# Graph layer on one core: one product for the vector part of z of two tiles, in front of both messages

## The chip, the cores and the metric

The kernel runs on one core of a Trainium2 chip. Its time is the device time of one execution in microseconds (us). "TensorE" is PE in the rows (its weight loads are PEld), "VectorE" is DVE, "ScalarE" is ACT, "GpSimd" is POOL; SP issues transfers. All data are 32-bit floats.

## The reference

One layer of a graph network over 50,000 nodes of 160 features (64 scalars and 32 vectors of 3) and 50,000 edges, sorted by their destination, then a residual and a layer norm:

```python
h = silu(edge_scalars @ (Wfc1 / sqrt(FC_IN)));  w = h @ (Wfc2 / sqrt(FC_H))   # w0..w3 per edge
e0 = f0[edge_src];  e1 = f1[edge_src]           # node features through Wl1_0, Wl1_1
mid0 = w0 * e0 * sh0
mid1 = w3 * einsum('eum,em->eu', e1, sh1) / sqrt(3.0)
mid2 = w1[:, :, None] * e0[:, :, None] * sh1[:, None, :]
mid3 = w2[:, :, None] * e1 * sh0[:, :, None]
# means over the edges of each destination, n0..n3
alpha = scal @ Wa * a * inv96
out_s = scal @ Wl2_s * a * inv96
out_v = einsum('num,uv->nvm', vec, Wl2_v) * a[..., None] * inv96
x = layernorm(x + sc + alpha * concat(out_s, out_v))
```

The kernel applies the last matrices per edge, ahead of the means. The message of an edge has 161 numbers: its share of alpha, 64 scalars and 96 numbers of the vectors. The vectors' share with sh1 is one row of 32 numbers times the three components of sh1: that is the vector part of z.

## The kernel before, in words

The first stage makes the messages. A tile is 128 edges, one on each partition; two tiles (t = 0, 1) are a pair (k), two pairs are a quad (q), 98 quads in all. Step d of the stage works on several quads at once, each engine in its own fixed order, with semaphores between the engines:

- GpSimd gathers the node rows of quad d, four indirect transfers (L587), each pair's behind the transposes of the quad four steps back that read the same slot of `gat`.
- TensorE: `first_layer(d)` (L670), `turn(d, 0)` (transposes, L676 and L678), `combine(d-3, 0)`, `turn(d, 1)`, `combine(d-3, 1)`, then `weigh(d-1)`. `combine` makes y of a pair, for each tile a product at L733 and one at L736, tile 0 first. `weigh` makes e (L696, L702) and w (L715).
- ScalarE: for each pair `take_turned(d, k)` (h_sb at L830, t_sb at L832) and `take_second(d-3, k)`, which copies 65 numbers of y of each tile to z (L840), one copy for each tile. At the end it copies e to e_sb (L855).
- VectorE: `multiply(d-2, 0)` (mid = w times e_sb, L977), `label(d-3)` (L985), `finish(d-3, 0)`, `multiply(d-2, 1)`, `finish(d-3, 1)`, `prepare(d+2)` (L952, L961, L967), and in some steps one small operation that prepares the second stage (`between`).
- SP stores the messages of each quad to DRAM.

`finish(q, k)` makes the messages of a pair. For each tile it waits for ScalarE's copy, writes the other 96 numbers of z (L995) and adds z to y times sh0 (L1001), which is the message. `y` of pair 0 lies in PSUM banks 2 and 3, which are also those of e, so `weigh` has these waits in front of L696:

```python
pe.wait_ge(t_out, 2 * q + 2)
for t in range(2):
    if q >= 2:
        pe.wait_ge(msg_ready[t], 2 * (q - 2) + 1)
    if q >= 1:
        pe.wait_ge(e_out[t], q)
```

`y` of pair 1 has banks of its own. z has one slot for each of the four tiles of a quad, `msg` two halves of a quad each.

The second stage takes the nodes in 98 groups of 512. For each it loads the windows of messages from DRAM, sums them by destination with one-hot matrices (L795), and adds the node's own product, the residual and the norm. Its first loads are issued by SP during the first stage, the others as the groups advance.

Of the kernel before, what the change touches and what calls it, by code (L numbers as in the profile page):

```python
# [22 lines left out]
P = 128  # L23
F32 = mybir.dt.float32
I32 = mybir.dt.int32
ALU = mybir.AluOpType
# [3 lines left out]
MUL0, MUL1 = 64, 32  # L30
# [65 lines left out]
def gnn_kernel(nc, turned, spread, x_g, src_t, dst_t, dst_rows, sh_t, ea_t, weights, out):  # L96
# [22 lines left out]
    with ExitStack() as ctx:  # L119
        def sb(name, shape, dt=F32):  # L120
            return ctx.enter_context(nc.sbuf_tensor(name, shape, dt))

        def sem(name):
            return ctx.enter_context(nc.semaphore(name))
# [54 lines left out]
        sha = sb("sha", [P, SHA_RING, QUAD, 4])  # L179
# [5 lines left out]
        z = sb("z", [P, 2, 2, 1 + D])  # L185
# [106 lines left out]
        mid_ready = [sem(f"mid_ready{t}") for t in range(2)]  # L292
        y_ready = [sem(f"y_ready{t}") for t in range(2)]
        zc_ready = [sem(f"zc_ready{t}") for t in range(2)]
        zb_ready = [sem(f"zb_ready{t}") for t in range(2)]
        label_ready = sem("label_ready")
        msg_ready = [sem(f"msg_ready{t}") for t in range(2)]
        messages_out = [sem(f"messages_out{h}") for h in range(2)]
# [634 lines left out]
        def _(dve):  # L933
# [54 lines left out]
            def finish(q, k):  # L988
                p, ring, y = 2 * q + k, q % SHA_RING, y_ps[k]
                for t in range(2):  # L990
                    n = 2 * k + t
                    dve.wait_ge(zc_ready[t], p + 1)
                    if p >= 2:
                        dve.wait_ge(msg_ready[t], p - 1)
                    nc.vector.tensor_tensor(  # L995
                        z[:, k, t, 1 + MUL0:].rearrange("p (m v) -> p m v", m=3),
                        y[:, t, 0:MUL1].unsqueeze(1).broadcast_to([P, 3, MUL1]),
                        sha[:, ring, n, 1:4].unsqueeze(2).broadcast_to([P, 3, MUL1]),
                        ALU.mult).then_inc(zb_ready[t], 1)
                    dve.wait_ge(zb_ready[t], p + 1)  # L1000
                    nc.vector.scalar_tensor_tensor(  # L1001
                        out=msg[:, q % 2 * QUAD + n, 0:1 + D], in0=y[:, t, Y_A:Y_C],
                        scalar=sha[:, ring, n, 0:1], in1=z[:, k, t, :],
                        op0=ALU.mult, op1=ALU.add).then_inc(msg_ready[t], 1)

            def step(d):
                if alive(d, 2):
                    multiply(d - 2, 0)
                if alive(d, 3):
                    label(d - 3)  # L1010
                    finish(d - 3, 0)
                if alive(d, 2):
                    multiply(d - 2, 1)
                if alive(d, 3):
                    finish(d - 3, 1)
                if alive(d, -AHEAD):
                    prepare(d + AHEAD)
# [459 lines left out]
```

## Time and the profile before

| | us |
|---|---|
| median of 3 runs (lowest, highest) | 932.42 (932.19, 933.69) |
| the profiled execution | 932.28 |
| its span in the trace | 930.5 |

The profiled execution is one run of the program; all rows are of it. Times in rows are counted from the start of its span. The first stage fills about 550 us of it, the second the rest. In a timeline each row is a start, a duration, the engine, the line and the operation; in brackets stands how long the engine was idle before it and what ended that.

### The profile page before, as it was taken

How to read it: one execution, taken by the hardware profiler on the slowest of the kernel's cores; microseconds unless marked ns; L12 is line 12 of the kernel's file. 1: busy time of each engine (PE TensorE's matmuls, PEld its weight loads, DVE VectorE, ACT ScalarE, POOL GpSimd, SP SyncE). 2: the span in 40 equal slices, each digit the busy share in tenths (PEclk: the TensorE clock that was granted, in tenths of full speed). 3: DMA queues.
4: the chain of work that ended last, by engine and by line, in shares of the span. 5: the costliest groups of instructions: out<-in, count | busy, mean ns of one | idle time of the engine just before them, and what ended most of it. 6: DMA issues, size and time to landing. Idle time of an engine off the chain costs nothing.

```text
span 930.5 us, 27956 instructions
## 1 busy us (share of the span) xinstructions
PE 880.9 (95%) x8336; PEld 758.5 (82%) x8336; DVE 812.1 (87%) x2797; ACT 632.5 (68%) x1961; POOL 714.5 (77%) x804
## 2 busy tenths in 40 slices
PE   3899999999999999999999889999999999999995
PEld 2778887888877878888888779989999898899994
DVE  3789999999988999999999978888888888888887
ACT  1555555555654555565565547888988888988887
POOL 6777777777777776777777318989998888989894
PEclk9999999999999999999999999999999999999998
DMA  6465554455565555456544227999999999999993
GB/s 181 118 178 159 163 143 127 133 140 131 140 133 133 168 156 150 132 160 181 153 131 133 86 84 231 305 305 302 303 302 301 300 304 295 300 306 308 304 298 136
DMA packets 87522, 186.47 MB, mean 200 GB/s; under 512 B 17647, under 2 KB 48139, under 8 KB 87372
## 3 DMA queue, kind: packets, MB, share of 16 engines
q1 hardware_dynamic: 48411, 87.72, 29.1%
q10 hardware_dynamic: 20016, 61.15, 19.7%
q0 software_dynamic: 18944, 35.81, 17.8%
q8 instruction: 69, 1.13, 0.5%
q14 instruction: 82, 0.66, 0.2%
HBM read 119.66 MB, written 64.95 MB: 198 GB/s over the span
## 4 chain that ended last, share of the span: by engine, by line
PE 46%; POOL 22%; issue 17%; DVE 11%; DMA 3%; ACT 1%; POOLq 0%; DVEq 0%; ACTq 0%
PE ps L795 7%; POOL res L640 7%; PE ps L736 7%; POOL gat L587 6%; PE ps L715 5%; POOL xa L628 5%; PE ps L733 4%; PE ps L805 4%; PE ps L696 4%; PE ps L702 4%; DVE mid L977 3%; PE ps L678 3%; POOL xa L624 3%; DVE z L995 2%; DMA gat<-spread,srcs 2%
## 5 line engine op out<-in xcount | busy, mean ns | idle before, releaser
L587 POOL DMA_INDIRECT gat<-turned,srcs x196 | 190.8, 973 | 66.6 <-issue 61.8
L587 POOL DMA_INDIRECT gat<-spread,srcs x196 | 188.7, 963 | 61.8 <-issue 60.0
L855 ACT ACTIVATE e_sb<-ps 128x512 f32<-128x512 f32 x196 | 106.4, 595 | 123.1 <-PE ps L702 122.0
L795 PE MATMUL ps<-win,hot 60*128 60x162 f32 x2352 | 189.1, 306 | 0.7 <-DVE hot L1318 0.7
L736 PE MATMUL ps<-wy,mid 128*128 128x161 f32 x784 | 182.3, 314 | 0.0
L795 PEld LDWEIGHTS ps<-win,hot 60*128 60x128 f32 x2352 | 164.9, 186 | 17.1 <-issue 16.5
L1001 DVE SCALAR_TENSOR_TENSOR msg<-ps,sha,z 128x161 f32<-128x161 f32 x392 | 151.0, 385 | 14.0
L640 POOL TENSOR_TENSOR res<-agg,pre 128x640 f32<-128x640 f32 x98 | 152.2, 1553 | 9.9 <-ACT agg L900 9.9
L733 PE MATMUL ps<-wy,mid 128*128 128x97 f32 x784 | 141.6, 262 | 0.2 <-DVE mid L977 0.2
L977 DVE TENSOR_TENSOR mid<-ps,e_sb 128x512 f32<-128x512 f32 x196 | 133.2, 680 | 2.2 <-PE ps L715 2.2
L878 ACT ACTIVATE fin<-res,shift,rstd 128x160 f32<-128x160 f32 x292 | 132.2, 539 | 1.3 <-DVE shift L1267 1.3
L900 ACT ACTIVATE agg<-ps,coef 128x160 f32<-128x160 f32 x392 | 122.8, 409 | 6.3 <-DVE coef L1358 6.2
L733 PEld LDWEIGHTS ps<-wy,mid 128*128 128x128 f32 x784 | 123.5, 191 | 1.3 <-issue 0.7
L840 ACT ACTIVATE z<-ps 128x65 f32<-128x65 f32 x392 | 89.7, 229 | 46.0 <-PE ps L736 45.5
L736 PEld LDWEIGHTS ps<-wy,mid 128*128 128x128 f32 x784 | 119.2, 192 | 0.0
L805 PE MATMUL ps<-wy,xt 128*128 128x128 f32 x784 | 113.5, 288 | 0.4 <-DVE pre L1345 0.4
L805 PEld LDWEIGHTS ps<-wy,xt 128*128 128x128 f32 x784 | 94.9, 191 | 17.7 <-issue 17.5
L995 DVE TENSOR_TENSOR z<-ps,sha 128x96 f32<-128x96 f32 x392 | 97.9, 250 | 9.1 <-ACT z L840 2.5
L830 ACT ACTIVATE h_sb<-ps 128x128 f32<-128x128 f32 x196 | 54.4, 278 | 74.3 <-PE ps L678 64.7
L715 PE MATMUL ps<-h_sb,wt 64*128 64x256 f32 x784 | 102.0, 379 | 1.4 <-DVE mid L977 1.4
L628 POOL TENSOR_TENSOR xa<-xin 128x512 f32<-128x512 f32 x98 | 102.8, 1048 | 0.0
L832 ACT ACTIVATE t_sb<-ps 128x384 f32<-128x384 f32 x196 | 95.0, 485 | 0.0
(104 smaller groups left out, 1543.2 us busy)
## 6 DMA issues: line engine op xcount, KB each, us to landing
win<-rows SPq DMA_DIRECT2D x392, 114.6 KB
rows<-msg SPq DMA_DIRECT2D x98, 326.0 KB
out<-fin ACTq DMA_DIRECT2D x47, 640.0 KB, 5.4
xin<-x_g ACTq DMA_DIRECT2D x92, 322.0 KB, 4.4
gat<-turned,srcs POOLq DMA_INDIRECT x196
gat<-spread,srcs POOLq DMA_INDIRECT x196
eas<-ea_t SPq DMA_DIRECT2D x7, 384.0 KB, 4.8
xin<-x_g SPq DMA_DIRECT2D x6, 322.0 KB, 4.2
```

The source lines that it names most:

```text
L587: pool.indirect_dma_start(out=gat[:, slot, first:first + of.shape[1]], out_offset=None, in_=of, in_offset=bass.IndirectOffsetOnAxis(ap=src ...
L628: nc.gpsimd.tensor_tensor(xa[:, b0, 0:GROUP, :], xin[:, n, :, 1:1 + P], xin[:, n, :, 0:1].broadcast_to([P, GROUP, P]), ALU.mult).then_inc( ...
L640: nc.gpsimd.tensor_tensor(res[:, slot], agg[:, b3], pre[:, b3], ALU.add).then_inc(res_ready, 1)
L715: last = nc.tensor.matmul(w_ps[:, t, 2 * c * P:2 * (c + 1) * P], wt[half, w:w + P], h_sb[half, b].rearrange("p k e -> p (k e)"), start=Tru ...
L733: nc.tensor.matmul(y[:, t, 0:W_Y1 - W_YA], mid[:, q % 2, t, 0, k, :], wy[:, 0:W_Y1 - W_YA], start=True, stop=True)
L736: nc.tensor.matmul(y[:, t, W_Y1 - W_YA:YW], mid[:, q % 2, t, 1, k, :], wy[:, of:of + VEC + 1 + MUL0], start=True, stop=True).then_inc(y_re ...
L795: last = nc.tensor.matmul(agg_ps[b1][:, 2 * h + k, 0:SW], hot[side(h), b1, k, c, :], win[side(h), (b - 1) % RING, k, c, 0:SW], start=c == ...
L805: nc.tensor.matmul(sca_ps[:, k, :], xt[:, b1, k, :], wy[:, W_SA - W_YA:W_SB - W_YA], start=True, stop=True)
L878: last = nc.scalar.activation(fin[:, past, k, :], res[:, past, k, :], ACT.Identity, bias=shift[:, past, k:k + 1], scale=rstd[:, past, k:k ...
L900: last = nc.scalar.activation(agg[:, b0, k, :], agg_ps[b0][:, k, 1:1 + D], ACT.Copy, scale=coef[:, b0, k:k + 1])
L977: nc.vector.tensor_tensor(mid[:, q % 2, t].rearrange("p c k e -> p (c k e)"), w_ps[:, t], e_sb[:, t], ALU.mult).then_inc(mid_ready[t], 1)
L1001: nc.vector.scalar_tensor_tensor(out=msg[:, q % 2 * QUAD + n, 0:1 + D], in0=y[:, t, Y_A:Y_C], scalar=sha[:, ring, n, 0:1], in1=z[:, k, t, ...
```

## The change

The two products that write the vector part of z, one for each tile, become one product over both tiles of a pair. It stands behind the waits for both of ScalarE's copies and in front of both messages. The semaphore that told of each product, one for each tile, becomes one for both.

```diff
-        zb_ready = [sem(f"zb_ready{t}") for t in range(2)]
+        zb_ready = sem("zb_ready")
...
                 for t in range(2):
-                    n = 2 * k + t
                     dve.wait_ge(zc_ready[t], p + 1)
                     if p >= 2:
                         dve.wait_ge(msg_ready[t], p - 1)
-                    nc.vector.tensor_tensor(
-                        z[:, k, t, 1 + MUL0:].rearrange("p (m v) -> p m v", m=3),
-                        y[:, t, 0:MUL1].unsqueeze(1).broadcast_to([P, 3, MUL1]),
-                        sha[:, ring, n, 1:4].unsqueeze(2).broadcast_to([P, 3, MUL1]),
-                        ALU.mult).then_inc(zb_ready[t], 1)
-                    dve.wait_ge(zb_ready[t], p + 1)
+                nc.vector.tensor_tensor(
+                    z[:, k, :, 1 + MUL0:].rearrange("p t (m v) -> p t m v", m=3),
+                    y[:, :, 0:MUL1].unsqueeze(2).broadcast_to([P, 2, 3, MUL1]),
+                    sha[:, ring, 2 * k:2 * k + 2, 1:4].unsqueeze(3).broadcast_to([P, 2, 3, MUL1]),
+                    ALU.mult).then_inc(zb_ready, 1)
+                for t in range(2):
+                    n = 2 * k + t
+                    dve.wait_ge(zb_ready, p + 1)
                     nc.vector.scalar_tensor_tensor(
                         out=msg[:, q % 2 * QUAD + n, 0:1 + D], in0=y[:, t, Y_A:Y_C],
```

## Rows read from the trace of the kernel before

**Rows 1.** The page, part 1: busy time, share of the span and instructions.

```profile
PE 880.9 (95%) x8336; PEld 758.5 (82%) x8336; DVE 812.1 (87%) x2797; ACT 632.5 (68%) x1961; POOL 714.5 (77%) x804
```

**Rows 2.** The table by stretches: PE, PEld, DVE, ACT, POOL, clock, DMA share, GB/s.

```profile
300.00:400.00 100.00, 97.39 (x870) 81.29 (x868) 93.23 (x273) 58.38 (x190) 72.71 (x76) 1.00 0.54 152
```

**Rows 3.** The waits of the first stage: us in total, times, longest.

```profile
PEld ps L696 <- ACT t_sb L832: 29.3, 90, 0.7
DVE sha L952 <- DMA gat<-spread,srcs: 21.2, 9, 11.6
PE ps L696 <- DVE msg L1001: 12.8, 25, 2.2
```

**Rows 4.** The timeline of VectorE in an ordinary step, label to mid.

```profile
301.70 0.17 DVE L985 COPY msg<-dsts 128x4 f32<-128x4 f32 x1
302.01 0.26 DVE L995 TENSOR_TENSOR z<-ps,sha 128x96 f32<-128x96 f32 x1
302.31 0.39 DVE L1001 SCALAR_TENSOR_TENSOR msg<-ps,sha,z 128x161 f32<-128x161 f32 x1
302.61 0.25 DVE L995 TENSOR_TENSOR z<-ps,sha 128x96 f32<-128x96 f32 x1
302.89 0.38 DVE L1001 SCALAR_TENSOR_TENSOR msg<-ps,sha,z 128x161 f32<-128x161 f32 x1
303.19 0.68 DVE L977 TENSOR_TENSOR mid<-ps,e_sb 128x512 f32<-128x512 f32 x1
```

**Rows 5.** The timeline of TensorE in the same step, and the next L696.

```profile
301.69 0.47 PE L736 MATMUL ps<-wy,mid 128*128 128x161 f32 x2
302.00 0.27 PE L676 MATMUL ps<-ident,gat 128*128 128x128 f32 x1
...
303.02 0.47 PE L736 MATMUL ps<-wy,mid 128*128 128x161 f32 x2
303.53 0.66 PE L696 MATMUL ps<-t_sb,wt 64*64 64x256 f32 x8
...
308.75 0.66 PE L696 MATMUL ps<-t_sb,wt 64*64 64x256 f32 x8
```

**Rows 6.** The timeline of ScalarE: copies of pair 0, last copy of pair 1.

```profile
301.75 0.23 ACT L840 ACTIVATE z<-ps 128x65 f32<-128x65 f32 x1
302.20 0.23 ACT L840 ACTIVATE z<-ps 128x65 f32<-128x65 f32 x1 [0.22 <-PE ps L736]
...
308.74 0.23 ACT L840 ACTIVATE z<-ps 128x65 f32<-128x65 f32 x1 [0.22 <-PE ps L736]
```

**Rows 7.** The timeline of VectorE in a longer step.

```profile
328.52 0.15 DVE L985 COPY msg<-dsts 128x4 f32<-128x4 f32 x1
328.59 0.24 DVE L995 TENSOR_TENSOR z<-ps,sha 128x96 f32<-128x96 f32 x1
...
329.45 0.38 DVE L1001 SCALAR_TENSOR_TENSOR msg<-ps,sha,z 128x161 f32<-128x161 f32 x1
```

**Rows 8.** The timeline of TensorE, the L696 of that step.

```profile
330.09 0.66 PE L696 MATMUL ps<-t_sb,wt 64*64 64x256 f32 x8 [0.27 <-DVE msg L1001]
```

**Rows 9.** The timeline of ScalarE, the last t_sb ahead of it.

```profile
329.03 0.48 ACT L832 ACTIVATE t_sb<-ps 128x384 f32<-128x384 f32 x1
```

**Rows 10.** The timeline of GpSimd: the gather behind the longer gap, and another.

```profile
301.98 0.94 POOL L587 DMA_INDIRECT gat<-turned,srcs  x1 [0.52 <-issue]
303.23 0.95 POOL L587 DMA_INDIRECT gat<-spread,srcs  x1 [0.30 <-issue]
```

**Rows 11.** The timeline of TensorE: first regular and last L696, 95 steps apart.

```profile
33.80 0.66 PE L696 MATMUL ps<-t_sb,wt 64*64 64x256 f32 x8 [1.13 <-DVE msg L1001]
...
542.04 0.66 PE L696 MATMUL ps<-t_sb,wt 64*64 64x256 f32 x8 [0.32 <-DVE msg L1001]
```

**Rows 12.** Groups by line and shape, 200 to 300 us: busy us, mean ns.

```profile
L961 DVE TENSOR_TENSOR qprod<-gat,sha 128x384 f32<-128x384 f32 x18 | 10.0, 558 | 2.2 <-DVE sha L952 0.5
```

**Rows 13.** The table by stretches, behind a gather that landed late.

```profile
281.00:286.00 5.00, 4.94 (x33) 4.00 (x34) 3.50 (x10) 1.72 (x4) 3.48 (x4) 0.66 0.54 141
```

## The prediction

> **What bounds the kernel now.** I read the page first. TensorE is busy for 95% of the span, VectorE for 87%, GpSimd for 77% [rows 1], which names no bound: the kernel has two stages with different limits. The table by stretches shows that the change lies wholly in the first, where in 300 to 400 us TensorE is busy 97.4, VectorE 93.2 and GpSimd 72.7 of 100 us, with the clock granted in full [rows 2]. Three nearly full engines need the question which wait ends last, so I went to the waits. In the first stage almost all of TensorE's waits stand before one line, L696, the start of the second-layer products `weigh` [rows 3]: its weight load waits 90 times, 29.3 us in all, put down to ScalarE's `t_sb`; its matmul waits 25 times, 12.8 us, for VectorE's `msg`.
>
> Which of the two is it? The timelines settle that. In an ordinary step the second message of `finish(q, 0)` starts at 302.89 and takes 0.38, so it ends at 303.27 [rows 4]; L696 starts at 303.53 [rows 5], 0.26 later. In a longer step the message ends at 329.45 + 0.38 = 329.83 [rows 7] and L696 starts at 330.09 [rows 8], again 0.26 later, while `t_sb` had ended at 329.03 + 0.48 = 329.51 [rows 9], 0.58 before. The distance to the message is constant, so L696 always waits for the message, also where the profile names `t_sb`: `e` shares its PSUM banks with `y` of pair 0, and `weigh` waits until both messages of pair 0 have read it.
>
> Now the loop that sets a step. TensorE needs 0.31 from the start of a pair of L736 to its next instruction (301.69 to 302.00), and the last pair in front of L696 starts at 303.02 [rows 5], so L696 could begin at 303.33; TensorE stands idle for 0.20. VectorE waits as well: the label copy starts at 301.70 and z of tile 0 only at 302.01, 0.31 later, just behind ScalarE's copy that ends at 301.75 + 0.23 = 301.98 [rows 4, 6]. In the longer step, where VectorE has other work in front, the same two are 0.07 apart (328.52 to 328.59) [rows 7]. So VectorE waits 0.24 of every ordinary step for ScalarE, ScalarE waits for TensorE's combine, and TensorE waits 0.20 for VectorE's messages. No engine is the bound; a loop through three of them is, and it is 308.75 - 303.53 = 5.22 us long [rows 5]. VectorE's own work is 5.22 - 0.24 = 4.98 a step, TensorE's 5.22 - 0.20 = 5.02. GpSimd's four gathers stand 1.25 apart and one of them has 0.52 before it instead of 0.30, so it needs 5.22 - 0.22 = 5.00 [rows 10].
>
> Between the first regular L696 at 33.80 and the last at 542.04 [rows 11] there are 95 steps. Counted there: 62 of about 5.22 (the loop), one of 4.66 at the end, 20 between 5.25 and 5.46 with a mean of 5.39 and 7 up to 5.62 with a mean of 5.54 (steps where VectorE prepares the second stage), and 5 longer ones, mostly behind gathers that landed late.
>
> **The change part by part.** Every pair of tiles now has two z products of 96 numbers, each directly in front of its message. They become one product of 192, with both messages behind it.
>
> VectorE's occupancy. Now z, msg, z, msg start at 302.01, 302.31, 302.61, 302.89 and the next operation at 303.19: 1.18 for a pair [rows 4]. The trace has no z of 192. Below it lies z of 96 with 0.25 to 0.26 [rows 4]; above it twice that, 0.50, since one operation shouldn't cost more than the two it replaces; between them the product of 384 numbers with a broadcast factor and the same kind of four-dimensional pattern takes 558 ns [rows 12]. From 250 to 558 ns for 288 more numbers is 1.07 ns each, so 96 more give 0.25 + 0.10 = 0.35. I take 0.35: one operation and its rows on both sides agree with one slope. The first message starts about 0.04 after z has ended (302.01 + 0.26 to 302.31 [rows 4]), the second, which has nothing to wait for, 0.30 after the first, as the z behind a message does now (302.31 to 302.61), and the next operation 0.30 later again: 0.39 + 0.30 + 0.30 = 0.99 in place of 1.18. That is 0.19 less for a pair, 0.38 for a step, and VectorE's own time falls from 4.98 to 4.60. If the second message were held until the first has ended it would start 0.385 behind it, not 0.30; no row shows a message directly behind a message, so this stays as an upper bound of 0.09 a step.
>
> The Trainium skill speaks for this bound: VectorE: DVE Perf Modes, "The DRAIN you can't avoid", has the next operation wait until the pipeline is empty, and only excepts operations that are not held. The rows have the next operation start before the last one's end (302.31 + 0.39 = 302.70 against 302.61 [rows 4]), so I go by the rows; by the rule without its exception the sum would be 95 times 0.09, some 8 us, higher.
>
> The wait that it adds. The product now needs the copies of both tiles. ScalarE's copy of tile 0 ends at 301.98, that of tile 1 starts at 302.20, after 0.22 of waiting for TensorE's combine of tile 1, and ends at 302.20 + 0.23 = 302.43 [rows 5, 6]. VectorE is through with the label at about 301.77, so the start of z moves from 302.01 to 302.46. What is queued behind it on VectorE is both messages of pair 0, then `mid` and pair 1; for the messages TensorE waits at L696. From the end of the copy of tile 1 to L696 it is now 303.53 - 302.43 = 1.10. After: 0.03 to the start of z, 0.35 of z, 0.04, 0.30 between the messages, 0.38 of the second, 0.26 to L696, 1.36 in all. The loop closes through this copy, because the copy follows TensorE's combine (L736 of tile 1 at 301.69 [rows 5]), which follows the last L696 in TensorE's own order with no wait between. So the loop becomes 5.22 + 0.26 = 5.48.
>
> Pair 1 costs nothing. Its second copy is ready 308.74 + 0.23 - 303.53 = 5.44 after the L696 of the step before [rows 5, 6], its z can only start about 5.74 after it, behind the later `mid`; the 0.19 saved there vanishes in VectorE's wait for pair 0, which grows to some 0.9. `mid` itself starts 0.26 later against ScalarE and TensorE of the same step, and its readers are a step away. GpSimd follows TensorE's transposes and gets 0.48 of slack instead of 0.22, SP's stores get more time. The one z semaphore instead of two adds no wait: both messages wait for the same product.
>
> The sum: 62 steps x 0.26 = 16.1. In 20 steps 5.48 - 5.39 = 0.09 each, 1.8: there VectorE's extra work now hides in its own longer wait (4.60 plus at most 0.6 of extra stays below 5.48). In 7 steps 5.48 - 5.54, -0.4. In the five long ones a gather has up to half a us more lead, so I take -1, with ends of 0 and -3. The last quads, where the loop is open, +0.3. Together +16.8 us. The second stage starts when the messages are done and its queue of loads is released by the same step counters, so it moves as a whole. Against the profiled execution of 932.28 us (span 930.5), which stands 0.14 below the median of 932.42, that is 949.1; forecast 949 us.
>
> **Rivals.** (a) Forecast: the loop grows by what the second copy costs less what the fused product saves, 949 us, between 940 (z of 0.25) and 957 (second message held). Chance 0.80.
>
> (b) Faster: VectorE's occupancy is what sets the step, and 0.38 of it goes. Then the step falls until TensorE's 5.02 ends it: -0.20 x 95 = -19, 913 us. For it: VectorE is busy 93%, and the longer steps are its own. Against it: the 0.24 before z in every ordinary step. It decides if the second copy is ready before VectorE arrives, which needs it 0.66 earlier than the rows have it. Chance 0.07. This is where a rule of the Trainium skill stands, VectorE: DVE Perf Modes, "Rules for kernel authors": with chained operations it is their number that is to be kept small, not the semaphores; this kernel would lose 196 of them. The trace doesn't contradict it for VectorE's time, only that this time sets the step.
>
> (c) No change: the copies close up. The balance is zero when the start of z moves by no more than the 0.19 that the fusion saves for pair 0; the rows have it move by 0.45. TensorE's two combines would have to stand closer than 0.5, and nothing in the change does that. 932 us, chance 0.04.
>
> (d) Worse: the held second message together with a z of 0.50, +0.24 more a step, or a lower TensorE clock from its longer idle of 0.46 a step. Behind the longest idle before L696, 2.2 us [rows 3], the mean granted clock of 281 to 286 us was 0.66 of 2.4 GHz [rows 13], between its two levels: those 5 us do the work of 3.3, so each such fall would cost 1.7 us, and ten of them 17. But the 90 idle times of 0.7 at most left the clock full where I looked [rows 2, 3]. 960 to 975 us, chance 0.09.
>
> **The numbers.** A change of less than 0.2% can't be told from none here. Slower holds (a) and (d), 0.89; faster 0.07; same 0.04. The range of 80% lies within the slower cases: 939 from z at 0.25 (10 us less) and 958 from the held message, which leaves out (b), (c), most of (d).
>
> **What would show it.** Steps of 5.48 between starts of L696 where they were 5.22, and the 5.4 ones gone; z of 128x192, some 350 ns, starting 0.03 behind the second copy; messages 0.30 apart; idle of 0.46 before L696, still 0.26 behind the message; VectorE's busy time down by about 196 x 0.15 = 29 us in a longer span. I am wrong if the copies of the two tiles end less than 0.2 apart or if z starts before the second copy's time of now.

## The result

The changed kernel took 965.29 us (median of 4, 963.58 to 968.11) against 932.35: a ratio of 1.034, 95% interval 1.031 to 1.038. It is slower by 33 us where 17 were forecast, and lies above the range of 939 to 958. The direction and the place were right, the size half of the real one. Its profiled execution took 965.73 us with a span of 964.0.

The page of the changed kernel, part 1, and the table by stretches, to be held against [rows 1, 2]:

```profile
PE 884.1 (92%) x8336; PEld 760.5 (79%) x8336; DVE 784.1 (81%) x2601; ACT 632.4 (66%) x1961; POOL 714.9 (74%) x804
```

```profile
300.00:400.00 100.00, 92.09 (x818) 77.14 (x816) 82.75 (x223) 55.37 (x179) 69.19 (x72) 1.00 0.53 146
...
582.00:592.00 10.00, 9.06 (x80) 8.16 (x79) 5.89 (x19) 2.66 (x8) 2.98 (x4) 0.83 0.39 117
```

VectorE does 28 us less work, as forecast, and the kernel is slower: every engine of the first stage is less busy. The waits of the first stage, against [rows 3]:

```profile
DVE z L994 <- ACT z L840: 77.4, 95, 2.5
...
PEld ps L696 <- ACT t_sb L832: 63.2, 93, 0.8
...
PE ps L696 <- DVE msg L1002: 46.7, 96, 1.7
```

VectorE now waits 95 times for ScalarE's copy, and TensorE's waits before L696, 29.3 and 12.8 us in the kernel before, have more than doubled. One step on VectorE, from the label to mid, against [rows 4]:

```profile
302.12 0.16 DVE L985 COPY msg<-dsts 128x4 f32<-128x4 f32 x1
303.23 0.36 DVE L994 TENSOR_TENSOR z<-ps,sha 128x192 f32<-128x192 f32 x1 [0.95 <-ACT z L840]
303.63 0.68 DVE L1002 SCALAR_TENSOR_TENSOR msg<-ps,sha,z 128x161 f32<-128x161 f32 x2
304.22 0.68 DVE L977 TENSOR_TENSOR mid<-ps,e_sb 128x512 f32<-128x512 f32 x1
```

The product of 192 takes 0.36, the messages follow at 0.40 and 0.30 and mid at 0.29: all as forecast. On ScalarE the copy of tile 1 and on TensorE two successive L696, against [rows 6, 5]:

```profile
302.81 0.23 ACT L840 ACTIVATE z<-ps 128x65 f32<-128x65 f32 x1 [0.22 <-PE ps L736]
```

```profile
304.56 0.66 PE L696 MATMUL ps<-t_sb,wt 64*64 64x256 f32 x8 [0.47 <-DVE msg L1002]
...
310.21 0.66 PE L696 MATMUL ps<-t_sb,wt 64*64 64x256 f32 x8 [0.47 <-DVE msg L1002]
```

The step is 5.64 or 5.65, and nearly all are alike: of the 95 steps behind the first regular L696, 92 lie between 5.63 and 5.72 and the longer steps of VectorE are gone. Forecast was 5.48. The missing 0.16 stands between two rows: the copy ends at 302.81 + 0.23 = 303.04 and z starts at 303.23, 0.19 later, where I had taken 0.03. The chain of waits shows what lies there (DVEq is VectorE's sequencer, which handles an instruction that does nothing but wait):

```profile
302.81 0.23 ACT z L840
303.04 0.03 issue
303.07 0.02 DVEq L991
303.09 0.05 issue
303.14 0.05 DVEq L993
303.19 0.04 issue
303.23 0.37 DVE z L994
```

The product has four semaphores to wait for. It carries the wait for one of them itself, that which the code names first, the copy of tile 0. The other three stand in two instructions in front of it. The one that ends last, the copy of tile 1, is in the first of these: it ends at 303.07, then the second has to be handled, then the product.

### The profile page after: what moved, and what is told of

Same layout as the page of the kernel before. It is cut to its first block, busy times and chain, and to the rows that moved or that the text cites. A ratio compares the mean times of both kernels' runs of the same rounds, so it can differ in the third digit from the quotient of the medians.

```text
span 964.0 us, 27762 instructions
## 1 busy us (share of the span) xinstructions
PE 884.1 (92%) x8336; PEld 760.5 (79%) x8336; DVE 784.1 (81%) x2601; ACT 632.4 (66%) x1961; POOL 714.9 (74%) x804
## 4 chain that ended last, share of the span: by engine, by line
PE 50%; issue 17%; POOL 17%; DVE 10%; ACT 3%; DMA 2%; DVEq 1%; POOLq 0%; ACTq 0%
PE ps L715 8%; POOL res L640 8%; PE ps L696 6%; PE ps L702 6%; PE ps L795 6%; PE ps L736 6%; POOL xa L628 5%; DVE msg L1002 5%; PE ps L733 4%; DVE z L994 4%; PE ps L805 4%; POOL xa L624 3%; PE ps L676 3%; ACT z L840 2%; PE ps L678 2%
## 5 line engine op out<-in xcount | busy, mean ns | idle before, releaser
L587 POOL DMA_INDIRECT gat<-turned,srcs x196 | 186.0, 949 | 90.8 <-PE ps L678 49.9
L587 POOL DMA_INDIRECT gat<-spread,srcs x196 | 194.6, 993 | 63.4 <-issue 59.8
L1002 DVE SCALAR_TENSOR_TENSOR msg<-ps,sha,z 128x161 f32<-128x161 f32 x392 | 132.8, 381 | 7.0
L994 DVE TENSOR_TENSOR z<-ps,sha 128x192 f32<-128x192 f32 x196 | 69.1, 353 | 77.9 <-ACT z L840 77.4
L696 PE MATMUL ps<-t_sb,wt 64*64 64x256 f32 x784 | 65.4, 401 | 46.7 <-DVE msg L1002 46.7
```

The source lines that it names most:

```text
L587: pool.indirect_dma_start(out=gat[:, slot, first:first + of.shape[1]], out_offset=None, in_=of, in_offset=bass.IndirectOffsetOnAxis(ap=src ...
L696: nc.tensor.matmul(e_ps[made, t, 2 * P:4 * P], wt[half, W_E1 + half.start:W_E1 + half.stop], t_sb[half, b, 1 + t].rearrange("p k e -> p (k ...
L1002: nc.vector.scalar_tensor_tensor(out=msg[:, q % 2 * QUAD + n, 0:1 + D], in0=y[:, t, Y_A:Y_C], scalar=sha[:, ring, n, 0:1], in1=z[:, k, t, ...
```

## The experiments

Each ratio is taken against runs of the kernel before on the same chip. The first four kernels ran on a chip where the kernel before took 1076.9 us (31 runs), and their own profiled steps were 6.5 to 6.7 long: in each of them ScalarE and VectorE have idle time that the profile puts down to no engine of the program ("remote"), ScalarE 118 to 187 us in all before its copies of e, VectorE 20 to 51 us before mid. I haven't found its cause. There another wait ends most steps, and the times of these runs say little of the loop; two of the kernels were run again elsewhere. Below, this is called the first chip.

**One wait.** One semaphore counts both copies of a pair; the product waits for it alone. The waits for earlier messages are covered, since ScalarE waits for them before it copies.

```diff
-                for t in range(2):
-                    dve.wait_ge(zc_ready[t], p + 1)
-                    if p >= 2:
-                        dve.wait_ge(msg_ready[t], p - 1)
+                dve.wait_ge(zc_ready, 2 * p + 2)
```

> The changed kernel with one semaphore for both copies of a pair, so that the product of 192 has a single wait, which it carries itself, instead of four of which three stand in two instructions of their own in front of it. Theory A (the product starts 0.19 behind the second copy instead of 0.03 because the wait that ends last stands in an instruction of its own, with another behind it): z starts 0.03 behind the copy, the step falls by 0.16 from 5.64 to 5.48, 95 x 0.16 = 15 us less than 965, about 950. Theory B (the delay is that of the larger product itself, or of a VectorE that has been idle for 0.9, or of PSUM being read by ScalarE just before): z still 0.19 behind, step 5.64, 965 us.

Measured on the first chip: 1073.48 us, ratio 0.997 (0.994 to 1.001). Inconclusive for the time. The gap itself can be read there all the same. The chain of waits, and the same product on VectorE:

```profile
310.02 0.36 ACT z L840 x2
310.39 0.02 issue
310.41 0.37 DVE z L991
```

```profile
310.41 0.36 DVE L991 TENSOR_TENSOR z<-ps,sha 128x192 f32<-128x192 f32 x1 [1.62 <-ACT z L840]
```

With a single wait, which the product carries, z starts 0.02 to 0.03 behind the second copy, as theory A has it, although VectorE had been idle for 1.62.

**The order of the waits**, four waits as in the change, but those of tile 1 are named first:

```diff
-                for t in range(2):
+                for t in (1, 0):
                     dve.wait_ge(zc_ready[t], p + 1)
```

> The changed kernel with the same four waits, those of tile 1 named first, so that the product itself carries the wait for the copy of tile 1 and the three others stand in front. Theory A: as with one wait, z 0.03 behind the second copy, step 5.48, about 950 us, since the three others are over before. Theory C (it is the number of waits that costs, each some 0.04 to 0.05): no change, step 5.64, 965. Theory B: 965 as well.

On the first chip 1077.21 us, ratio 1.001 (0.997 to 1.005): inconclusive. In its trace there z starts 0.08 behind the second copy (304.70, 304.78) and not 0.03. The copies end 0.12 apart on that chip, and the wait for the first of them now stands in front with another behind it, 0.20 before z. Then, on a chip where the kernel before took 935.48:

> The changed kernel with the wait for the copy of tile 1 carried by the product, once more, since on the chip of the first four runs the kernel before took 1077 us with steps of 6.7 and the loop was another. Where the kernel before takes 932: theory A, z 0.03 behind the second copy, step 5.48, about 950 us (ratio 1.018); theories B and C, z 0.19 behind, step 5.64, 965 us (1.034).

Measured 949.10 us, ratio 1.015 (1.011 to 1.020). The chain of waits of this kernel, from the second copy to L696:

```profile
303.25 0.23 ACT z L840
303.48 0.02 issue
303.50 0.37 DVE z L994
303.87 0.03 issue
303.90 0.06 DVE msg L1002
303.96 0.24 issue
304.20 0.38 DVE msg L1002
304.58 0.24 issue
304.82 0.66 PE ps L696 x8
```

The instructions that only wait are out of the chain, z starts 0.02 behind the copy, and 91 of 95 steps lie between 5.46 and 5.48. The shape of the product, VectorE's idle of 0.78 before it, the number of waits and ScalarE's read of PSUM just before are all still there, so theories B and C fall; what counts is which wait the product itself carries. This is also the kernel that my prediction described. Its step of 5.47 is the forecast 5.48; its ratio of 1.015 holds the forecast 1.018 in its interval. That the time is 949 to the microsecond is partly luck: the kernel before took 935.48 on this chip, so the kernel is 13.6 us slower where 16.8 were forecast.

**The added wait without the fusion**: the kernel before, where the first product of a pair also waits for the second copy and carries that wait.

```diff
-                    dve.wait_ge(zc_ready[t], p + 1)
+                    dve.wait_ge(zc_ready[1], p + 1)
+                    if t == 0:
+                        dve.wait_ge(zc_ready[0], p + 1)
```

> The kernel before, two products of 96, but the first of a pair also waits for the copy of tile 1 (carried by the product itself). This is the added wait without the fusion. Theory A: the whole chain of pair 0 starts 302.46 - 302.01 = 0.45 later, step 5.22 + 0.45 = 5.67; 62 x 0.45 + 20 x 0.28 + 7 x 0.13 = 34 us more, about 966. The fusion is then worth 0.19 a step on the path. Rival: the fusion is worth nothing on the path and the wait is the whole cost; then this step equals that of the fused kernel with one wait, 5.48, 950 us.

On the first chip 1078.53 us, ratio 1.002 (0.999 to 1.005). Again on the other chip:

> The kernel before with the added wait and without the fusion, once more on another chip. Where the kernel before takes 932: if the fusion is worth 0.19 a step on the path, step 5.67, about 966 us (1.036); if it is worth nothing there, step 5.48, 950 us (1.018).

Measured 967.47 us, ratio 1.036 (1.032 to 1.040), on the same chip as the 949.10. Its timeline of TensorE:

```profile
400.23 0.66 PE L696 MATMUL ps<-t_sb,wt 64*64 64x256 f32 x8 [0.49 <-DVE msg L1003]
405.89 0.66 PE L696 MATMUL ps<-t_sb,wt 64*64 64x256 f32 x8 [0.49 <-DVE msg L1003]
```

The step is 5.66. So the later start costs 0.44 a step and the fusion gives 0.19 back (5.66 against 5.47), as worked out in the prediction.

**Only pair 1 fused**, pair 0 as before.

> Only pair 1 fused (with the wait for the copy of tile 1 carried by the product), pair 0 as before. If only pair 0 closes the loop: ordinary steps stay at 5.22, VectorE's own time falls from 4.98 to 4.79, and the 27 longer steps, which it sets, lose up to 0.19 each: about 4 to 5 us less than 932, 928. Rival: pair 1 is on the loop too, then the ordinary step grows above 5.22 and the kernel is slower than 932.

On the first chip 1079.61 us, ratio 1.003 (1.001 to 1.006), where a gain was expected; with the other wait at work there it says nothing of the loop. Pair 1 fused with no other change was run nowhere else; a pair of kernels below, both with another order of TensorE's waits, answers the question.

**TensorE waits for each message apart**: in the kernel before, e of tile 0 is made behind the message of tile 0, and only then TensorE waits for that of tile 1.

```diff
                 for t in range(2):
...
-                for n in range(2):
-                    for t in range(2):
+                    for n in range(2):
```

> The kernel before, but TensorE makes e of tile 0 behind the message of tile 0 and only then waits for that of tile 1, so that the loop closes through the first message. If the loop is what I say, L696 no longer waits: the step falls from 5.22 to TensorE's own 5.02; the longer steps, VectorE's own, stay. 62 x 0.20 = 12 us less, 920. Rival: the weight loads in the new order cost more than they give, or GpSimd's 5.00 makes gathers late: 930 to 935.

Measured 1031.53 us, ratio 1.102 (1.097 to 1.107). The forecast for this kernel fell, for a reason beside the question: to wait in between, I had put the products of one tile together. The rival named the place, though not the size. The timeline of TensorE of this kernel, then that of its weight loads:

```profile
299.17 0.65 PE L695 MATMUL ps<-t_sb,wt 64*64 64x256 f32 x4
299.75 0.70 PE L700 MATMUL ps<-t_sb,wt 64*128 64x256 f32 x2
300.38 0.65 PE L695 MATMUL ps<-t_sb,wt 64*64 64x256 f32 x4
```

```profile
299.75 0.29 PEld L700 LDWEIGHTS ps<-t_sb,wt 64*128 64x128 f32 x2 [0.39 <-issue]
300.38 0.19 PEld L695 LDWEIGHTS ps<-t_sb,wt 64*64 64x64 f32 x4 [0.33 <-issue]
300.95 0.18 PEld L700 LDWEIGHTS ps<-t_sb,wt 64*128 64x128 f32 x1 [0.39 <-issue]
```

Four records of L695, half of the work, now stand 0.58 ahead of what follows; in the changed kernel, where the tiles alternate, all eight take 0.60 (304.56 to 305.16). The step is 6.29. TensorEngine Tiling (Array Packing) in the Trainium skill, "Gotcha 1: PSUM Pressure", says that products in different rows of the array can't use the same PSUM bank at once; the two halves n of one tile do just that. The trace doesn't show that this is the cause. The two records of L700, one product alone, take 0.63 (299.75 to 300.38) where the kernel before needs about 0.54 for all four (304.12 to 304.66): half the work didn't shorten this group either. What both kinds of group have in common is the change of shape between them, 64*64 and 64*128. At each such change the weight loads stand idle for 0.33 to 0.39, once within e in the kernel before and three times here. That is a rival which no run sets apart from the bank.

**The same with pair 1 fused:**

> As the one before, and pair 1 fused as the change does it, pair 0 not. VectorE's own time falls by 0.19 a step, so the longer steps shorten as well: 20 x 0.37 and 7 x 0.4 less at most, together with 62 x 0.20 between 15 and 22 us less than 932, about 914. Rival: no gain over the split alone (920), if the longer steps aren't VectorE's own.

Measured 1025.73 us, ratio 1.099 (1.095 to 1.102), with the same step of 6.29: a miss for the same reason.

**The two waits of the kernel before, swapped.** Nothing else is changed: the product of 96 then carries the wait that is long over.

```diff
-                    dve.wait_ge(zc_ready[t], p + 1)
                     if p >= 2:
                         dve.wait_ge(msg_ready[t], p - 1)
+                    dve.wait_ge(zc_ready[t], p + 1)
```

> The kernel before with the two waits in front of each product of 96 named in the other order: the product then carries the one that is long over, and the wait for ScalarE's copy stands in an instruction of its own. Nothing else changes. If such an instruction costs 0.02 and 0.05 to the next, as in the trace after, z starts 0.10 behind the copy instead of 0.03, once a step on the path: ordinary steps 5.22 + 0.08 = 5.30, 62 x 0.08 = 5 us more, a ratio of 1.005. Rival: the cost is only there behind a long idle of VectorE: no change.

Measured 939.37 us against 933.73 on its chip, ratio 1.005 (1.002 to 1.007). From its timelines, VectorE and ScalarE:

```profile
402.03 0.16 DVE L985 COPY msg<-dsts 128x4 f32<-128x4 f32 x1
402.40 0.26 DVE L995 TENSOR_TENSOR z<-ps,sha 128x96 f32<-128x96 f32 x1 [0.21 <-ACT z L840]
```

```profile
402.07 0.23 ACT L840 ACTIVATE z<-ps 128x65 f32<-128x65 f32 x1
```

The copy ends at 402.30 and z starts at 402.40, 0.10 behind, in place of 0.03 [rows 4, 6]; the ordinary step is 5.29. One instruction that only waits costs 0.07, two cost 0.16, with no other change to the kernel, and behind an idle of 0.21 as well as of 0.95.

**TensorE's waits in another order**: the kernel before, with the waits for the messages named first, that of tile 1 ahead.

```diff
-                pe.wait_ge(t_out, 2 * q + 2)
-                for t in range(2):
+                for t in (1, 0):
                     if q >= 2:
                         pe.wait_ge(msg_ready[t], 2 * (q - 2) + 1)
+                pe.wait_ge(t_out, 2 * q + 2)
+                for t in range(2):
                     if q >= 1:
                         pe.wait_ge(e_out[t], q)
```

> The kernel before with the five waits in front of L696 in another order, so that the first weight load carries the wait for the second message of pair 0, which ends last, and the others stand in front. Now two waiting instructions lie between that message and the load, which starts 0.22 behind the message's end. If each costs what those on VectorE cost, L696 starts 0.04 to 0.08 behind the message, the ordinary step falls from 5.22 to about 5.04, next to TensorE's own 5.02: 62 x 0.18 = 11 us less, a ratio of 0.988. The longer steps, VectorE's own, stay. Rival: TensorE's 0.25 is its own start-up and not the waits': no change.

Measured 928.05 us, ratio 0.993 (0.991 to 0.996). Its timelines, VectorE and TensorE (L697 is the L696 of before):

```profile
404.04 0.38 DVE L1002 SCALAR_TENSOR_TENSOR msg<-ps,sha,z 128x161 f32<-128x161 f32 x1
```

```profile
404.56 0.66 PE L697 MATMUL ps<-t_sb,wt 64*64 64x256 f32 x8
...
409.67 0.66 PE L697 MATMUL ps<-t_sb,wt 64*64 64x256 f32 x8
```

The message ends at 404.42 and L697 starts 0.14 later, in place of 0.26; the step is 5.11. The gain is 0.11 a step where 0.18 was expected. It isn't the effect that is smaller; the loop has ceased to set the step. TensorE stands idle no longer, as the last product in front of L697 and the table by stretches show:

```profile
404.17 0.47 PE L737 MATMUL ps<-wy,mid 128*128 128x161 f32 x2
```

```profile
400.00:450.00 50.00, 50.00 (x452) 42.33 (x449) 47.03 (x138) 30.21 (x98) 38.11 (x40) 1.00 0.65 176
```

From the start of the last pair of L737 to L697 it is 0.39, where it was 0.51 in the kernel before (303.02 to 303.53) [rows 5]. In the kernel of the two separate waits it is 0.39 as well (298.78 to 299.17), although the message of tile 0, for which it waits, had ended at 298.07 + 0.39 = 298.46, 0.71 before. So 0.39 is TensorE's own, the prediction's 0.31 was read in front of a transpose, and in the kernel before TensorE waits 0.51 - 0.39 = 0.12 and not 0.20. Its own step is 5.22 - 0.12 = 5.10, and this kernel's ordinary steps are 5.10 or 5.11. What the order of the waits is worth while the loop still sets the step, the last kernel below shows.

**Pair 1 fused and TensorE's waits in that order:**

> As the one before, and pair 1 fused as the change does it (its product carries the wait for the second copy), pair 0 as before. If pair 1 is off the loop and the longer steps are VectorE's own, they fall by up to 0.19 each beside the gain of the first: 27 x 0.19 = 5 us more gain, a ratio of 0.983. Rival: no difference to the one before, or pair 1's wait shows and it is slower than that.

Measured 924.77 us, ratio 0.990 (0.988 to 0.993), on the same chip as the one before. Two of VectorE's longer steps, first in the kernel with TensorE's order alone, then with pair 1 fused as well:

```profile
331.03 0.66 PE L697 MATMUL ps<-t_sb,wt 64*64 64x256 f32 x8 [0.26 <-DVE msg L1002]
336.47 0.66 PE L697 MATMUL ps<-t_sb,wt 64*64 64x256 f32 x8 [0.27 <-DVE msg L1002]
```

```profile
327.49 0.66 PE L698 MATMUL ps<-t_sb,wt 64*64 64x256 f32 x8
332.73 0.66 PE L698 MATMUL ps<-t_sb,wt 64*64 64x256 f32 x8
```

5.44 and 5.24: these steps lose 0.2, the ordinary ones stay at 5.11. The medians lie 3.3 us apart where 5 were expected; four runs each, which overlap (925.09 to 931.70, 922.98 to 926.63), don't set that apart from noise, so the gain of pair 1 rests on the steps. Against the kernel before the version is faster clear of noise, by 1.0%.

**Both orders mended in the whole change:**

> The whole change with both orders of waits mended: the product carries the wait for the second copy, the first weight load of L696 that for the second message. The step is 5.47 - 0.18 = 5.29 throughout, against 5.22 for 62 and 5.39 for 20 and 5.54 for 7 before: 62 x 0.07 - 20 x 0.10 - 7 x 0.25 = about +1 us, a ratio of 1.001. With the fusion of pair 0 there is nothing to win even then.

Measured 937.16 us, ratio 1.004 (1.002 to 1.006), with steps of 5.27 or 5.28. Its chain of waits from the first message of pair 0 to L697:

```profile
407.61 0.07 DVE msg L1003
407.68 0.24 issue
407.92 0.39 DVE msg L1003
408.30 0.04 issue
408.35 0.66 PE ps L697 x8
```

Here the loop still sets the step, and L697 starts 0.05 behind the message in place of 0.26; the step falls from 5.47 to 5.27. So the two instructions that only wait cost 0.21 in front of L696, more than on VectorE. Even with every wait where it costs least, fusing pair 0 doesn't pay: the kernel before this one, which differs from it by pair 0 alone, took 924.77 on the same chip.

## Why the prediction was right and wrong

- What bounds: a loop through three engines and not the busiest of them. Right. VectorE lost 28 us of work and the kernel grew by 33; and wherever a link of this loop was moved and the loop went on setting the step, the step moved by about as much (0.42, 0.25, 0.44, 0.07 and 0.20). That L696 doesn't wait for `t_sb` has a simpler reason than the one I gave: `weigh(d-1)` reads the `t_sb` of the quad before, which was made a step earlier, and not the one whose end I compared.
- The product of 192 at 0.35 and the messages 0.30 apart: 0.36 (a mean of 353 ns on the page), and 0.30. Right. The second message isn't held. The fusion gives 0.19 a step, shown by the pair of kernels with the same wait, with and without it.
- The start of z 0.45 later behind the second copy: 0.44 a step with the wait carried. Right.
- "After: 0.03 to the start of z". This is the step that failed. It was 0.19, so the loop grew by 0.42 and not by 0.26. Over 95 steps the 0.16 are 15 us, and mending it alone brought the ratio from 1.034 to 1.015, a kernel of 949.10 on its chip. I read 0.03 from a product that carries the deciding wait itself and applied it to one that doesn't. No bound of the range held this: I had bounded every duration, and not the gap in front of the product, and I wrote that the single z semaphore adds no wait without counting the waits that the product collects from both tiles. The rows gave a hint that I passed over: VectorE's product started 0.03 behind its releaser [rows 4, 6], TensorE's L696 0.26 behind its own [rows 4, 5]. Five waits stand in front of L696, and 0.21 of that 0.26 was this same cost: with the load carrying the wait it is 0.05.
- The sum. The 95 steps add up to 508.24 us before and 538.40 after, 30.2 more. The forecast's own classes with 5.64 give 62 x 0.42 + 20 x 0.25 + 7 x 0.10 = 31.7, and the long steps behind late gathers, which became fewer, take off about 2. The other 3.3 of the span's 33.5 stand behind the last L696: from there to the end it is 391.9 in place of 388.5. In 582 to 592 us the granted clock was 0.83, and the first sums of windows took 2.94 in place of 1.93. The rest of it I haven't traced; the runs of the changed kernel differ by 4.5 among themselves.
- Pair 1 costs nothing. Right: with and without its fusion the ordinary steps are 5.11 in the kernels that settle it.
- TensorE's own 5.02 and its 0.20 of idle time: both mis-sized, without an effect on the forecast. They are 5.10 and 0.12, since the product in front of L696 needs 0.39 and not 0.31; rival (b) would have gained 0.12 a step and not 0.20.
- The rivals: (b) and (c) didn't come. (d) named a z of 0.50, a slower clock and a held message; none was the cause, and that its 960 to 975 us hold the measured 965 is luck.

## What to carry to other kernels

When an instruction has to wait for more than one semaphore, find out which wait ends last and see that the instruction itself carries that one; each instruction that only waits, between the end of that wait and the work, cost 0.07 to 0.1 us here, every time on the path. Two constant gaps of different size behind a releaser (0.03 and 0.26) are a question to ask before one of them goes into a sum. Fusing two operations pays where their inputs are both ready when the engine arrives and the engine's own time sets the step, as for pair 1 in the longer steps, and costs the distance between the inputs where they set the pace, as for pair 0.

## What the runs showed of the hardware

- The rule by which the wait is placed, as these kernels show it: the semaphore named first in the code is carried by the instruction, the others go to one or two instructions in front. Perfetto Trace Analysis in the Trainium skill, "Identifying Dependency Chains", notes that such instructions may be inserted, and the chains of these traces show them (DVEq L991 and L993). Here two cost 0.16 and one 0.07 on VectorE, and two in front of a weight load 0.21 on TensorE.
- With the products of one tile put together, TensorE needed 0.58 for four records of e where alternating tiles needed 0.60 for eight, and 0.63 for two where they needed 0.54 for four. Whether it is the shared bank, the order of the halves or the change of shape between the groups was not taken apart.
- The same kernel before took 932 to 936 us in three of the groups of runs and 1077 in a fourth, on the first chip. There the added wait, which costs 3.6% elsewhere, made a ratio of 1.002: a loop of waits can be measured only where it sets the step.
